# Last stage's fill: the key rotations of the first three sequences move from POOL to DVE

## The reference

```python
for i in range(DEPTH):                                  # DEPTH = 6
    x = attn_layer(shift_tokens(x), Wqkv[i], q_scale[i], k_scale[i], Wo[i]) + x
    x = ffn_layer(shift_tokens(x), ...) + x

# attn_layer, 16 heads of 64, local windows of 32
q, k, v = jnp.split(x @ Wqkv, 3, -1)
q = l2norm(q) * qs
k = l2norm(k) * ksc
q = q * cos * scale + rotate_half(q) * sin * scale      # the rotation of the queries
k = k * cos * inv + rotate_half(k) * sin * inv          # the rotation of the keys
out = local_attention(q, k, v)                          # softmax over 64 keys per query
return out @ Wo
```

## Time and profile before

| | us |
|---|---|
| median of 3 runs | 4821.71 |
| lowest and highest run | 4821.47, 4842.27 |
| the profiled execution's own time | 4826.14 |
| its span | 4824.8 |
| start of L3f in the span | 1574.7 |
| busy: PE, DVE, ACT, POOL | 4585.6, 3684.2, 3495.8, 3661.4 |

### The profile page before, as it was taken

How to read it: one execution, slowest core, us unless ns; L and a number is a source line. 1 busy time by engine, 2 the same in 40 slices (tenths; PEclk the granted TensorE clock), 3 DMA queues, 4 the chain that set the end, 5 groups by cost and what they waited for, 6 DMA issues and landing times.

```text
span 4824.8 us, 115181 instructions
## 1 busy us (share of the span) xinstructions
PE 4585.6 (95%) x44704; PEld 3135.6 (65%) x44704; DVE 3684.2 (76%) x5130; ACT 3495.8 (72%) x6738; POOL 3661.4 (76%) x2336
## 2 busy tenths in 40 slices
PE   7998999997887799999999999999999999999997
PEld 5665768874444466666666666666666666666665
DVE  4553457667999688888888888888888888888885
ACT  3443765556776588888888888888888888888885
POOL 1111334448998899999999999999999999999993
PEclk9998999998999999999999999999999999999998
DMA  2000000003342222232223322223223322322222
GB/s 78 1 2 1 2 1 1 1 1 141 154 163 106 50 57 62 67 75 65 68 53 78 76 61 58 66 69 72 68 55 75 73 55 67 80 60 66 60 57 51
DMA packets 164147, 289.00 MB, mean 60 GB/s; under 512 B 44047, under 2 KB 61206, under 8 KB 159510
## 3 DMA queue, kind: packets, MB, share of 16 engines
q1 hardware_dynamic: 162310, 281.46, 22.2%
q10 hardware_dynamic: 1296, 0.18, 0.0%
HBM read 90.16 MB, written 2.62 MB: 19 GB/s over the span
## 4 chain that ended last, share of the span: by engine, by line
PE 59%; ACT 3%; issue 2%; DVE 2%; POOL 1%; ACTq 0%; DVEq 0%; POOLq 0%
PE ps L2544 18%; PE ps L2599 8%; PE ps L2573 8%; PE ps L2557 7%; PE ps L2612 6%; PE ps L2586 3%; PE ps L2654 3%; PE ps L2645 3%; PE ps L2638 3%; ACT L3f_pT L2805 2%; PE ps L2619 1%; PE ps L2625 1%; ACT L3f_kT L2788 1%; ACT L3f_qz L2784 0%; DVE L3f_rot L2427 0%
## 5 line engine op out<-in xcount | busy, mean ns | idle before, releaser
L3140 POOL TENSOR_TENSOR L3f_t<-L3f_raw,L3f_rot 128x512 f32<-128x512 f32 x768 | 1007.3, 1334 | 276.2 <-DVE L3f_raw L2956 276.2
L2544 PE MATMUL ps<-L3f_wqkv,all_z 128*128 128x512 f32 x2304 | 1134.3, 601 | 12.9 <-DVE L3f_raw L2956 11.7
L3157 POOL TENSOR_TENSOR L3f_raw<-L3f_raw,L3f_t 128x1024 f32<-128x1024 f32 x384 | 960.6, 2502 | 3.8
L3149 POOL TENSOR_TENSOR L3f_raw<-L3f_raw,L3f_rot 128x1024 f32<-128x1024 f32 x384 | 954.0, 2484 | 3.8
L2956 DVE TENSOR_TENSOR L3f_raw<-ps,L3f_ri 128x512 f32<-128x512 f32 x768 | 495.3, 681 | 233.1 <-ACT L3f_ri L2763 231.6
L2939 DVE TENSOR_REDUCE L3f_ss<-L3f_sqr 128x8 f32<-128x512 f32 x768 | 507.6, 681 | 162.2 <-ACT L3f_sqr L2753 159.6
L2557 PEld LDWEIGHTS ps<-all_ident,L3f_raw 128*128 128x128 f32 x3072 | 358.9, 141 | 318.2 <-issue 283.4
L2544 PEld LDWEIGHTS ps<-L3f_wqkv,all_z 128*128 128x128 f32 x2304 | 385.5, 191 | 221.4 <-issue 152.3
L2557 PE MATMUL ps<-all_ident,L3f_raw 128*128 128x128 f32 x3072 | 472.2, 276 | 46.9 <-ACT L3f_kT L2788 27.1
L2805 ACT ACTIVATE L3f_pT<-ps 64x512 f32<-64x512 f32 x768 | 453.2, 590 | 85.8 <-PE ps L2586 77.9
L2753 ACT ACTIVATE L3f_sqr<-ps 128x512 f32<-128x512 f32 x768 | 449.9, 599 | 76.4 <-PE ps L2544 71.5
(11 more groups left out here) (336 smaller groups left out, 8634.2 us busy)
## 6 DMA issues: line engine op xcount, KB each, us to landing
L3f_vw<-L3f_v SPq DMA_DIRECT2D x1344, 128.0 KB, 2.4
L3a_Bs<-L3a_rows SPq DMA_DIRECT2D x16, 2048.0 KB, 7.1
L3a_Cs<-L3a_rows SPq DMA_DIRECT2D x16, 2048.0 KB, 11.7
L3f_vw<-L3f_v SPq DMA_DIRECT2D x192, 64.0 KB, 2.1
L3f_wqkv<-in_L_ffn_Wqkv SPq DMA_DIRECT2D x24, 256.0 KB, 2.8
L3f_wqkv<-in_L_ffn_Wqkv SPq DMA_DIRECT2D x6, 512.0 KB, 3.6
L3f_wo<-in_L_ffn_Wo SPq DMA_DIRECT2D x48, 64.0 KB, 2.3
out<-all_x SPq DMA_DIRECT2D x8, 256.0 KB, 3.1
```

What stands on the lines that cost most here:

```text
L2544: p.matmul(PS[:, j % 3, :], Z[:, u % NSEQ, t * P:t * P + P], w, start=True, stop=True).then_inc(proj.sem)
L3140: op = g.tensor_tensor(t[:, :, to], r[:, :, fr], w[:, 1, to].unsqueeze(1).broadcast_to((P, H, WIN)), ALU.mult)
L3149: g.tensor_tensor(r, r, w[:, 0, :].unsqueeze(1).broadcast_to((P, H, HD)), ALU.mult).then_inc(cosined.sem)
L3157: g.tensor_tensor(r, r, t, ALU.add).then_inc(rotated.sem)
```

## The change

For the units 0, 1 and 2 (`EARLY = 3`) the key halves k0 and k1 are rotated by DVE, in a new step `rotate` behind the second `norm` of the half. It issues two instructions of 128x512, then 128x1024 twice, with the same operands as POOL's three steps. POOL keeps the rotations of the queries; in the places of the key halves it waits once for `k_rotated` and then writes one element per partition of a new tile `done` three times, to raise its three semaphores. All other units stay as they were.

```diff
--- before.py
+++ after.py
@@ -2343,6 +2343,7 @@
         UH = UNIT // HD
         N = DEPTH * NSEQ
         FINAL = NSEQ // 2
+        EARLY = 3
         pre = "L3_ffn_"
 
         wqkv = self.sb("wqkv", [P, 3 * INNER])
@@ -2358,6 +2359,7 @@
         lmaskb = self.sb("lmaskb", [P, TILES, 2, KEYS], BF16)
         mean = self.sb("mean", [P, P])
         cmat = self.sb("cmat", [P, P])
+        done = self.sb("done", [P, 3, 1])
         ss = self.sb("ss", [P, 2, TILES * 4 * UH])
         floor = ss[:, 1, :]
 
@@ -2471,6 +2473,7 @@
         proj, sqr_in, ss_in, ss_max, ss_ln, ss_rs, normed, v_out, *v_put = self.signals(
             "proj:12", "sqr_in:8", "ss_in:8", "ss_max:4", "ss_ln:4", "ss_rs:4", "normed:8", "v_out:4", f"v_put0:{16 * 4 * NW}", f"v_put1:{16 * 4 * NW}")
         sined, cosined, rotated = self.signals("sined:4", "cosined:4", "rotated:4")
+        k_sined, k_cosined, k_rotated = self.signals("k_sined:2", "k_cosined:2", "k_rotated:2")
         qk_turned, qk_in, scored, s_mask, s_max, s_sub, s_exp, s_sum, s_inv, s_mul = self.signals(
             "qk_turned:8", "qk_in:8", "scored:2", "s_mask:2", "s_max:2", "s_sub:2", "s_exp:2", "s_sum:2", "s_inv:2", "s_mul:2")
         p_turned, pT_in, o_mm, oT_in, w_mm, z_attn = self.signals("p_turned:2", "pT_in:2", "o_mm:2", "oT_in:2", "w_mm", "z_attn")
@@ -2926,6 +2929,15 @@
             exponent(2 * i + 3, 1)
             length(2 * i + 4, "k1")
 
+        def half_of(u, x):
+
+            c = "qk".index(x[0])
+            return heads(raw[:, int(x[1]), c * INNER:(c + 1) * INNER]), heads(t2[:, c, :]), rot[:, u // NSEQ % 2, int(x[1]), 2 * c:2 * c + 2, :]
+
+        def early(u, x):
+
+            return u < EARLY and x[0] == "k"
+
         def dve(i):
             v = nc.vector
 
@@ -2955,6 +2967,26 @@
                     v.wait_ge(*qk_turned.at(u - 1, i))
                 v.tensor_tensor(heads(raw[:, t, g * UNIT:(g + 1) * UNIT]), heads(PS[:, RING.index(x) % 3, :]),
                                 ri[:, i * UH:(i + 1) * UH].unsqueeze(2).broadcast_to((P, UH, HD)), ALU.mult).then_inc(normed.sem)
+
+            def rotate(u, x):
+                if not 0 <= u < N or not early(u, x):
+                    return
+                n = int(x[1])
+                r, t, w = half_of(u, x)
+                v.wait_ge(*normed.at(u, 2 * HALF.index(x) + 1))
+                v.wait_ge(*rot_in.at(0))
+                if n:
+                    v.wait_ge(*k_rotated.at(u, 0))
+                elif u:
+                    v.wait_ge(*k_rotated.at(u - 1, 1))
+                for half in range(2):
+                    to, fr = slice(half * WIN, (half + 1) * WIN), slice((1 - half) * WIN, (2 - half) * WIN)
+                    op = v.tensor_tensor(t[:, :, to], r[:, :, fr], w[:, 1, to].unsqueeze(1).broadcast_to((P, H, WIN)), ALU.mult)
+                op.then_inc(k_sined.sem)
+                v.wait_ge(*k_sined.at(u, n))
+                v.tensor_tensor(r, r, w[:, 0, :].unsqueeze(1).broadcast_to((P, H, HD)), ALU.mult).then_inc(k_cosined.sem)
+                v.wait_ge(*k_cosined.at(u, n))
+                v.tensor_tensor(r, r, t, ALU.add).then_inc(k_rotated.sem)
 
             def sc():
                 return PS[:, 6:8, :].rearrange("p b (a k) -> p (b a) k", k=KEYS)
@@ -3046,6 +3078,7 @@
             share(2 * i + 1, 1)
             norm(2 * i + 2, "k1a")
             norm(2 * i + 2, "k1b")
+            rotate(2 * i + 2, "k1")
             scale(2 * i + 1, 0)
             residual(2 * i)
             gated(2 * i - 1, 0)
@@ -3066,6 +3099,7 @@
             bounded(2 * i + 3, "k0")
             norm(2 * i + 3, "k0a")
             norm(2 * i + 3, "k0b")
+            rotate(2 * i + 3, "k0")
             hidden(2 * i + 2, 0)
             top(2 * i + 2, 0)
             sums(2 * i + 3, "q1a")
@@ -3079,6 +3113,7 @@
             bounded(2 * i + 3, "k1")
             norm(2 * i + 3, "k1a")
             norm(2 * i + 3, "k1b")
+            rotate(2 * i + 3, "k1")
             hidden(2 * i + 2, 1)
             top(2 * i + 2, 1)
             total(2 * i + 2, 0)
@@ -3099,6 +3134,7 @@
             normal(2 * i + 1)
             norm(2 * i + 4, "k0a")
             norm(2 * i + 4, "k0b")
+            rotate(2 * i + 4, "k0")
             scale(2 * i + 2, 1)
             hidden(2 * i + 3, 0)
             top(2 * i + 3, 0)
@@ -3119,14 +3155,14 @@
         def pool(i):
             g = nc.gpsimd
 
-            def half_of(u, x):
-                c = "qk".index(x[0])
-                return heads(raw[:, int(x[1]), c * INNER:(c + 1) * INNER]), heads(t2[:, c, :]), rot[:, u // NSEQ % 2, int(x[1]), 2 * c:2 * c + 2, :]
-
             def sine(u, x):
                 if not 0 <= u < N:
                     return
                 i = HALF.index(x)
+                if early(u, x):
+                    g.wait_ge(*k_rotated.at(u, int(x[1])))
+                    g.memset(done[:, 0, :], 1.0).then_inc(sined.sem)
+                    return
                 r, t, w = half_of(u, x)
                 if u % NSEQ == 0 and i == 0:
                     g.wait_ge(*rot_in.at(u // NSEQ))
@@ -3144,6 +3180,9 @@
                 if not 0 <= u < N:
                     return
                 i = HALF.index(x)
+                if early(u, x):
+                    g.memset(done[:, 1, :], 1.0).then_inc(cosined.sem)
+                    return
                 r, t, w = half_of(u, x)
                 g.wait_ge(*sined.at(u, i))
                 g.tensor_tensor(r, r, w[:, 0, :].unsqueeze(1).broadcast_to((P, H, HD)), ALU.mult).then_inc(cosined.sem)
@@ -3152,6 +3191,9 @@
                 if not 0 <= u < N:
                     return
                 i = HALF.index(x)
+                if early(u, x):
+                    g.memset(done[:, 2, :], 1.0).then_inc(rotated.sem)
+                    return
                 r, t, w = half_of(u, x)
                 g.wait_ge(*cosined.at(u, i))
                 g.tensor_tensor(r, r, t, ALU.add).then_inc(rotated.sem)
```

## The result

| | before | after |
|---|---|---|
| median of 12 runs each, us | 4821.77 | 4831.65 |
| the profiled execution's own time, us | 4826.14 | 4830.12 |
| its span, us | 4824.8 | 4828.8 |
| busy in the span: PE, DVE, ACT, POOL, us | 4585.6, 3684.2, 3495.8, 3661.4 | 4585.3, 3698.2, 3495.8, 3618.0 |

The ratio of the runs is 1.0017, with an interval of 1.0010 to 1.0024: some 8 us slower (4.8 to 11.6), which lies within the 0.5% that was called "same". The medians differ by 9.9 us. POOL gave up 43.4 us of work, as the prediction had it; DVE took on 14.0 us net, for its 23 us of rotations came with 9 us less of being held up. PE's busy time over the whole span is what it was; in the fill it is longer, and in the stages ahead of it shorter.

What follows compares the result with a forecast made beforehand. PE bounds the last stage, so only the fill before its gapless run counts: 23 us of DVE rotations, nearly 17 given back by vanished waits, leave 6.3 us, 4828 us by the median; range 4809 to 4842.

Steps and rivals of the forecast that it cites:

- delay D: Along DVE's chain in the fill: the time of an instruction now less that before, ending at 6.3 us.
- the prediction's marker: Projection of k0b of unit 3 on PE, first piece behind the last gap, before at 1676.66 us; predicted 6.3 us later.
- The cost of a rotation: Four DVE instructions per key half: 1.29 + 1.22 + 1.22 + 0.1 = 3.8 us, six of them 23 us.
- Steps 1 to 4: Key rotations of units 0 and 1 on DVE: delays of 2.0, 4.6, 7.3 and 7.6 us.
- Step 5: DVE's scale of unit 0: 7.05 us of blocking by POOL gone, 1.7 come back, leaving a delay of 1.7 us.
- Step 7: Rotation of k1 of unit 2: DVE's idle wait absorbs about 1.1 us; delay 8.4 us at the residual of unit 0.
- Step 8: Scale of unit 1, no longer blocked by POOL: 3.31 becomes 1.22 us, delay 6.3 us at the norm of unit 3.
- POOL was the chain: Rival for the fill: rotations hidden on DVE, 12.9 us of POOL's cost come back, 4809 us; chance 0.18.
- Nothing comes back: Rival for the fill: six rotations lie on the chain in full, 24 us slower, 4846 us; chance 0.12.
- It cancels: Rival for the fill: the delay shrinks further where ACT is late, time unchanged at 4822 us; chance 0.10.
- Side by side: Rival: DVE's key and POOL's query rotations run together, +3 us, 4825; counted within the forecast's 0.60.
- DVE gets in only where POOL pauses: Reading of the 8.27 and 3.31 us scales: a DVE instruction with two SBUF operands waits until POOL itself pauses.

Runs made afterwards that it cites:

- cost: Kernel before, POOL still rotating everything, plus six unused DVE reduces totalling 22 us behind the key norms of units 0 to 2; ratio to before 1.0022.
- free: Changed kernel with POOL's add of a query half put ahead of its wait for DVE's key half; ratio to before 1.0036.
- late_free: Changed kernel with query adds ahead of the wait for keys and each DVE rotation one half later, behind the next query norm; ratio to before 1.0013.
- relief: Changed kernel with the DVE rotations left out, a one-column multiply per half in their place; ratio to before 0.9978.
- early1: Changed kernel with EARLY = 1, so only the two key halves of unit 0 are rotated by DVE; ratio to before 0.9995.
- early2: Changed kernel with EARLY = 2, so DVE rotates the keys of units 0 and 1, four rotations; ratio to before 1.0005.
- yield1: Kernel before with POOL's sine of q0 of unit 2 made to wait for the 8.27 us scale of unit 0; ratio to before 0.9998.
- mix: Changed kernel with EARLY = 1 and three added POOL waits for DVE scales of units 0 and 1; ratio to before 0.9988.
- the three nudges: Kernel before with a tiny DVE memset, three tiny POOL memsets, or a 512-column DVE reduce near the 8.27 us scale; ratios 0.9996, 1.0007, 0.9999.
- yield2: Kernel before with POOL's sine and cosine of q0 of unit 2 waiting for the first and second scale of unit 0; ratio to before 0.9985.

## Why the prediction was right

The forecast was 4828 us (range 4809 to 4842), "same" at 0.92; the median is 4831.65. Of the 3.7 us between them, 1.1 lie in the fill (7.4 instead of 6.3); the rest is below what the runs resolve (their interval for the change is 4.8 to 11.6 us). That 7.4 is so near to 6.3 is in part luck: several terms were off by 1 to 2 us and nearly cancel, as the steps show.

The delay D at each step, as predicted and as the two timelines show it (2.84 added to a time after):

| step | predicted | measured | at |
|---|---|---|---|
| 1, k0 of unit 0 | 2.0 | 1.75 | `sums`, 1588.70 |
| 2, k1 of unit 0 | 4.6 | 3.84 | `sums`, 1600.58 |
| 3, `norm` of unit 1, `hidden` | 3.4, 7.3 | 2.79, 6.63 | 1609.25, 1614.30 |
| 4, k1 of unit 1 | 7.6 | 7.46 | `hidden`, 1629.64 |
| 5, `norm` behind `scale` of unit 0 | 1.7 | 1.40 | 1645.04 |
| 6, k0 of unit 2 | 5.6 | 5.26 | `scale`, 1650.10 |
| 7, k1 of unit 2, residual | 8.4 | 7.48 | 1672.41 |
| 8, `norm` of unit 3 | 6.3 | 7.61 | 1680.68 |
| the prediction's marker, k0b of unit 3 on PE | 6.3 | 8.45 | 1682.27 |

- **The cost of a rotation** (3.8 us): 3.8 measured where it met nothing (1610.57 to 1614.38), 3.9 in the first. The first pair waited for POOL at steps 1 (0.08 us) and 2 (0.84), elsewhere not.
- **Steps 1 to 4** came out 0.1 to 0.8 us early. The wait of 0.4 us at step 4 did not come: there the pair took 1.29.
- **Step 5**, the gain, is the one on which the sum hung: 7.05 us of blocking gone, some 0.5 back (1.69 instead of 1.22; I had put 1.7). POOL's `cosine` ended where I had put it (1643.33 + 2.84 = 1646.2, I had 1646.3), but the `scale` was issued 1.0 us later than I had put it (D = 8.0 instead of 7), and so had less of it to wait for. The two errors cancel: D = 1.4 instead of 1.7.
- **Step 7** came 0.9 lower: 0.3 were carried over, and DVE's idle stretches on the way took up 1.6 us instead of 1.1 (D = 3.6 at the `norm` of 1666.29).
- **Step 8 is the term that was mis-sized.** I had D = 8.4 - 2.1 = 6.3. The subtraction was right on DVE, but D stood at 9.7 when this `scale` was issued (at 1679.44, before at 1672.58), not at the residual's 7.5. Behind PE's new wait of 4.8 us came slow rows on PE. Its timeline, before:

```profile
1668.66 0.70 PE L2619 MATMUL ps<-all_z,L3f_cmat 128*128 128x256 f32 x2 [0.94 <-DVE all_z L3007]
1669.20 1.88 PE L2544 MATMUL ps<-L3f_wqkv,all_z 128*128 128x512 f32 x4
```

and after:

```profile
1673.31 1.22 PE L2622 MATMUL ps<-all_z,L3f_cmat 128*128 128x256 f32 x2 [4.79 <-DVE all_z L3039]
1674.33 3.62 PE L2547 MATMUL ps<-L3f_wqkv,all_z 128*128 128x512 f32 x4
```

The same matmuls took 4.84 us instead of 2.58. Busy time by stretch, after, around them (columns as in the earlier trace rows; the clock is the last but two):

```profile
1668.00:1673.00 5.00, 0.52 (x2) 0.00 (x0) 4.92 (x7) 0.00 (x0) 1.58 (x2) 0.80 0.00 0
1673.00:1678.00 5.00, 4.69 (x8) 2.32 (x9) 0.94 (x2) 1.49 (x4) 1.77 (x3) 0.52 0.23 51
1678.00:1683.00 5.00, 3.51 (x18) 1.91 (x16) 3.29 (x5) 4.54 (x10) 0.95 (x1) 1.00 0.89 204
```

The granted clock is 0.52 from 1673 to 1678, about the 1.2 GHz level, behind a stretch in which PE did 0.52 us of work in 5; from 1678 on it is 1.00 again, 2.4 GHz. That is 2.26 us on the chain, and 7.48 + 2.26 = 9.74, against the 9.70 found. I had priced PE's gaps at their length only. The same matmuls are as slow in cost and free, behind gaps of 5.8 and 4.8 us, and at full speed in before and nine of the other kernels, behind 0.9 to 1.4 us; in late_free they are slow behind 1.4 us, so this one gap is not the whole of it.

  Nor did all of the 2.1 us of step 8 reach PE. The prediction's marker stands in PE's timeline after as

```profile
1682.27 1.02 PE L2547 MATMUL ps<-L3f_wqkv,all_z 128*128 128x512 f32 x2
```

  and the transposes ahead of it, which wait for a copy of ACT's in both kernels, still had D = 9.7 (1681.80, before 1674.94). Before, the projection waited 1.09 us more, for the `norm` behind the blocked `scale`; after, it came straight behind the transposes. So only 1.25 us came back there, and D was 8.45: at 1685.1 on the scale of before, where I had said near 1683. Between this marker and the scores 1.06 us more came back, as before had its own slow stretch there (clock 0.80 from 1673 to 1680, the two projection rows in 1.55 us against 1.02): 7.4. That last part I had not foreseen; at the marker that the prediction had named, the miss is 8.45 instead of 6.3.

- **The rate behind the fill** is unchanged, as predicted.
- **The rivals.** "POOL was the chain" is half true: relief shows its 12.9 us, the number worked out for it (3.7 + 7.05 + 2.1), and it is what the change gives where the rotation on DVE is free. It isn't. (That the tenth agrees is chance: in relief the `scale` still took 1.92 us, so 0.7 of the 7.05 was not given back there.) "Nothing comes back" (24 us) is refuted by the 7.4 itself, and early1, which has two rotations in it, is 3.2 us ahead of before. "It cancels" fits early2, not the change. "Side by side" is refuted by free, where the pair goes from 1.29 to 3.5 us as soon as POOL is at work.
- **A slip in the bounds**: a rotation with its first pair at 0.65 us and no gaps comes to 0.65 + 1.22 + 1.22 = 3.1 us, not 2.9, so the lower bound over six is -4 us, not -5. Nothing hung on it.
- **A reading that was wrong without harming the sum**: that DVE gets in only where POOL pauses. yield1 refutes it, and the trace before could have: I took a `scale` of 3.31 us at 1672.58, which got in at a pause of 0.08 us, for the same kind of block as the 8.27. From 1709 on there are 92 `scale`s that got in between two instructions of POOL's without a pause. The first, on DVE and on POOL:

```profile
1709.67 1.59 DVE L2999 TENSOR_TENSOR L3f_sm<-L3f_sm,L3f_sl 128x1024 f32<-128x1024 f32 x1
1710.12 3.37 POOL L3157 TENSOR_TENSOR L3f_raw<-L3f_raw,L3f_t 128x1024 f32<-128x1024 f32 x1
```

  POOL's `sine` ended at 1710.17, DVE went next, and the `add` was the one that waited (3.37 us instead of 2.35). The Trainium skill (SBUF — State Buffer, "Who interferes with whom") says that a DVE instruction with two SBUF inputs contends with a GpSimd instruction that reads SBUF, and calls it an exclusive lock, so that one waits out the other. This agrees with 150 of the 151 instructions of DVE with two SBUF operands that were issued in L3f before while one of POOL's had more than 0.05 us to go: they got in at its end. It does not agree with the one of 8.27 us. As the prediction's sum was built from the measured 8.27 and from waits of one instruction elsewhere, it came out.

The change as a whole: taking the work off POOL gives 13 us in the fill where nothing is added to DVE, and the same work on DVE takes more than that, as DVE's queue was already what the projections, the softmax and the residual wait for there. What shortened the fill was a little moved work near the start (early1), and letting DVE in at the one long block (yield1); mix has both.

## What to carry to other kernels

Moving work from one engine to another has two prices that can be measured apart: leave the work out (relief), and add it without taking it away (cost). Here they were -12.9 and +10.9 us and did not add up, because the added work alone already made the long block and the waits for POOL vanish, so the sum has to be carried step by step along one chain, with a delay that is shrunk by every idle stretch it crosses. Where instructions of two engines exclude each other, an idle stretch of the one off the chain is worth something: look at the longest instruction of a group (8.27 us where the median is 1.37) and let the other engine wait for it with one semaphore. And a gap of PE costs more than its length when the matmuls behind it run at the lower clock: here 4.8 us of gap and 2.3 more, though the same gap of 2.83 us was followed by 1.00 in one trace and by 0.50 in five. And a profile is one execution: where two of them are compared to a microsecond, look first at whether PE ran the same rows at the same clock.

## What the runs showed of the hardware

- One instruction of DVE can be passed over by several of POOL's in a row. The group of `scale` in the kernel before (instruction, count, shortest, median and longest in ns):

```profile
L2999 DVE TENSOR_TENSOR L3f_sm<-L3f_sm,L3f_sl x192: 1211/1365/8273, 1637.6 to 4772.3; 128x1024 f32<-128x1024 f32 x192
```

  191 of them waited for at most one instruction of POOL; the first took 8.27 us, and 5.79, 6.91, 7.05 and 6.34 in early1 and the three nudges, where it was issued at other points of POOL's instructions, and it always ended about 1.08 us behind the `cosine` of q0 of unit 2. It did not occur where POOL had to pause once near it (1.21 in yield1, 1.69 after), nor in cost, where DVE came later (1.57). The product of the rotation table was passed over by one instruction in 10 of 70 meetings. The cause is open.
- In an ordinary meeting the waits are shared out: the `scale` of 3.29 us in yield1 waited 2.1, and the POOL instruction behind it was 1.0 us longer. A dearer POOL row can be the trace of a DVE instruction that got in.
- The same rows of PE run at either speed from one profiled execution to the next: the two projection rows 58.5 to 58.9 us behind the `memset` took 1.02 us in before, at a granted clock of 1.00, and 1.91 or 1.92 in yield1, yield2 and the three nudges (0.50), whose edits come later, all of them behind a gap of 2.83 us of PE's, and the `scale` behind them was issued 1.2 to 1.3 us later. A shift of such size is no verdict on an edit before the rows ahead of it have been compared.
